# A four-stage layer kernel on one core: local attention with values stationary, Mamba's states by channel halves, a new plan

## Chip, cores, metric

One core of one Trainium2 chip. The metric is the device time of the whole program in microseconds, the median of the runs; lower is better. All times below are microseconds unless they say ns.

## What is computed

16 sequences of 256 tokens, width 128. After a layer norm, the first layer adds a Mamba block and a top-1 mixture of 8 experts to x; after a second layer norm, the second layer adds a 16-head attention with an arccos kernel ("g" units) and a two-deep local-attention transformer ("l" units). What the change touches, cut from the reference:

```python
# Mamba, per channel d (256) and state n (16), along the tokens
h = dA * h + dBx                      # dA = exp(dt*A), dBx = dt*B*x
y = jnp.einsum('bdn,bn->bd', h, c)    # sum over the 16 states
# local attention, 8 heads of 64, window 64, keys of the own and the previous window
sim = jnp.where(mask, -jnp.finfo(sim.dtype).max, jnp.einsum('bhwid,bhwjd->bhwij', bq, bk))
attn = jax.nn.softmax(sim, axis=-1)
out = jnp.einsum('bhwij,bhwjd->bhwid', attn, bv)
x = x + out_reshaped @ wo
```

## The kernel before

The sequences go in 8 pairs (index i or n); a pair has T = 512 tokens, TT = 4 tiles of 128. The work is cut into small units, each with a name: m_* is Mamba, e_* the experts, f_* their joining and second norm, g_* the arccos attention, and the names without a prefix (shift, qkv, norm, qn, heads, score, pt, pv, on, oT, wo, ln, up, gelu, hid, down) the local-attention layer, listed in LAYER. One instance of that layer is one sequence b of a pair in one of the two depths: 8 x 2 x 2 = 32 instances.

**The order.** schedule() is a list scheduler that runs at build time. STAGES gives each unit its engine times, all_units() its due time and what it comes after, LATER and STREAM shift the due times by unit name and by stream. The scheduler hands out the 8 PSUM banks (takes_banks, frees_banks), books a table load on ScalarE (ACT) when a unit needs another activation table (NEEDS, SWITCH), and writes a fixed order for each engine: PE, ACT, DVE, POOL and the DMA queue of SyncE (SP). Each engine then runs its list in order and waits on semaphores.

**Local attention** for one instance (L = 256 tokens, two 128-token tiles, 4 pairs k of heads, z the head of the pair):
- score (L1140, L1144, L1147): scores with queries on partitions. Per head one mask matmul with a bf16 identity, two 64x64 products and one 64x128 product. Four units of it. DVE takes the negative row maximum (L1684, nmx).
- pt (L1155, L1159, L1165, L1166): the same scores transposed, keys on partitions, 320 columns a head (SC). Per head one mask matmul, three products, and two matmuls that add the negative maximum: nmx broadcast as stationary operand, the identity as moving one, 128 and 192 columns. Four units. ACT takes the exponential into PT (L1426); there are two PT tiles for both sequences.
- pv (L1179 to L1181): one unit a head, three matmuls with the exponentials as stationary operand and 65 columns of vv moving: 64 values and a column of ones, which gives the row sum. Eight units.
- on (L1694, L1698): DVE takes the reciprocal of the sums and normalises into oo, three heads at a time.
- oT: eight transposes (L815, the transpose helper) and two ACT copies (L1429) into oT. Then wo (L1195).

**Mamba**, per pair 16 steps k: q, c = divmod(k, 2), so the two channel halves c alternate and q is a pair of states. m_ex (ACT, L1312), m_bx, m_scan, m_hc (DVE, L1530, L1536, L1542), m_sum (PE, L1013), which adds the transposed products into one bank for each half; both banks are taken at the first two steps and given back by m_turn at the end. SP fetches B and C rows, broadcast to 128 partitions, once for each q (512 KB each, L1887 and L1893, 8 + 8 for a pair), into two buffers each; a fetch waits until the steps of q - 2 have read the buffer.

Of the kernel before, what the change touches and what calls it, by code (L numbers as in the profile page):

```python
# [6 lines left out]
ALU = mybir.AluOpType  # L7
# [42 lines left out]
OH = 3  # L50
OG = -(-LH // OH)
# [21 lines left out]
    "g_out": [("PE", 0.89), ("DVE", 0.68)], "out": [("DVE", 0.69), ("SP", 0.1)], "zeros": [("DVE", 0.34)],  # L73
    "shift": [("PE", 0.22), ("ACT", 0.97)], "norm": [("DVE", 0.17), ("ACT", 0.5)], "qn": [("DVE", 1.22)], "heads": [("PE", 0.88), ("ACT", 1.03)],
    "score": [("PE", 1.0), ("DVE", 0.61)], "pt": [("PE", 2.32), ("ACT", 0.7)], "pv": [("PE", 0.64)], "on": [("DVE", 0.78)],
    "oT": [("PE", 0.44), ("ACT", 0.6)], "wo": [("PE", 1.83), ("DVE", 0.42)], "ln": [("PE", 0.69), ("DVE", 0.77), ("ACT", 0.54)],
# [12 lines left out]
         "norm": "ln", "pt": "ln", "ln": "ln", "m_in": "silu", "g_tan": "tan", "gelu": "gelu"}  # L89
SWITCH = 127.0  # L90

LATER = {"down": 9, "e_down": 27, "e_lg": -177, "e_ln": 421, "e_load": -1379, "e_place": 30, "e_pre": -533, "e_route": -824,
         "e_scat": 827, "e_store": -1322, "e_tr": 261, "e_up": 40, "e_xn": -205, "e_xt": -160, "f_ln": 337, "f_tr": -1175,
         "f_xn": 125, "f_yg": 758, "g_av": 86, "g_avT": -766, "g_ev": -1332, "g_hd": -30, "g_ln": 728, "g_norm": -329, "g_oT":
         355, "g_out": 176, "g_pow": 587, "g_qkv": 73, "g_score": 51, "g_sq": 85, "g_sub": 1181, "g_tan": 60, "gelu": -398,
         "heads": 45, "hid": -32, "l_weights": 124, "ln": -103, "ln2": 5, "lnT": -6, "m_B": 636, "m_C": -449, "m_bx": 56,
         "m_dt": 27, "m_du": -6, "m_ex": -11, "m_fin": 286, "m_hc": 82, "m_in": -32, "m_load": 285, "m_out": -1531, "m_scan":
         1342, "m_sum": 17, "m_turn": -313, "m_weights": -862, "m_xp": 1631, "norm": -9, "oT": -3, "on": -102, "out": 152,
         "pt": -29, "pv": 73, "qkv": 47, "qn": -92, "score": -1, "shift": -37, "up": -72, "wo": 32, "x_load": 78, "zeros": 451}

STREAM = {("e", 0): 131, ("e", 1): 87, ("e", 2): 61, ("e", 3): 65, ("e", 4): 580, ("e", 5): 193, ("e", 6): 235,
# [18 lines left out]
         "g_score": 2, "g_avT": 1, "g_oT": 1, "g_out": 1, "shift": 1, "qkv": 1, "heads": 2, "score": 2, "pt": 2, "oT": 1, "wo": 1, "ln": 1,  # L120
         "lnT": 1, "up": 1, "down": 1}
LAYER = ("shift qkv0 qkv2 qkv3 qkv5 norm qn0 heads0 qn1 heads1 score0 score1 pt0 pt1 pv0 pv1 pv2 on0 pv3 score2 score3 "
         "pt2 pt3 pv4 pv5 on1 pv6 pv7 on2 oT0 oT1 wo ln ln2 lnT up0 up1 up2 gelu hid0 hid1 hid2 down")
LAYER = [(x.rstrip("0123456789"), int(x[-1])) if x[-1].isdigit() and x != "ln2" else (x, 0) for x in LAYER.split()]


def durations(unit):
    u, n, b, k = unit
    if u == "e_xt" and n >= GJ[1]:
        return [("PE", 0.11), ("DVE", 0.22)]  # L130
    if u == "e_up" and n >= GJ[1]:
# [25 lines left out]
def all_units():  # L157
# [33 lines left out]
    for n in range(NPAIR):  # L191
# [11 lines left out]
        for q in range(NQ):  # L203
            last = CH * (q - 1) - 1
            unit(t0 + 10 + q, ("m_B", n, 0, q), ("m_xp", n), *[("m_bx", n, 0, last) for z in range(1) if q >= 2])
            unit(t0 + 10 + q, ("m_C", n, 0, q), ("m_xp", n), *[("m_hc", n, 0, last) for z in range(1) if q >= 2])
        for k in range(STEPS):
            q, c = divmod(k, CH)
            t2 = t1 + step * k
            unit(t2 - 4, ("m_ex", n, 0, k), ("m_du", n, 0, c), *[("m_scan", n, 0, k - 2) for z in range(1) if k >= 2])  # L210
            unit(t2, ("m_bx", n, 0, k), ("m_du", n, 0, 0), ("m_du", n, 0, 1), ("m_B", n, 0, q), *[("m_sum", n, 0, k - 2) for z in range(1) if k >= 2])
            unit(t2, ("m_scan", n, 0, k), ("m_bx", n, 0, k), ("m_ex", n, 0, k))
            unit(t2, ("m_hc", n, 0, k), ("m_scan", n, 0, k), ("m_C", n, 0, q))
# [3 lines left out]
        for c in range(CH):  # L217
            unit(t3, ("m_turn", n, 0, c), ("m_sum", n, 0, STEPS - 2 + c))
            unit(t3, ("m_fin", n, 0, c), ("m_turn", n, 0, c))
        unit(t3, ("m_out", n), ("m_fin", n, 0, 0), ("m_fin", n, 0, 1), ("x_load", n))  # L220

    for i in range(NPAIR):
# [45 lines left out]
        for b in range(2):  # L268
            for l in range(LAY):
                n = LAY * i + l  # L270
                for j, (u, k) in enumerate(LAYER):
                    t1 = start + PERIOD * (0.25 * b + 0.5 * l + 0.5 * j / len(LAYER))
                    x = [("zeros", 0, b)]
                    if u == "shift":
                        x = [("down", n - 1, b)] if l else [("f_xn", i)] + [("pt", n - 1, b, 3) for z in range(1) if n]
                    elif u == "qkv":
                        x = [("shift", n, b)] + [("down", n - 1, b) for z in range(1) if n] + [("pv", n - 1, b, 7) for z in range(1) if n and k % 3 == 2]
# [9 lines left out]
                    elif u == "pt":  # L287
                        x = [("score", n, b, k)] + [("pt", n, b, k - 1) for z in range(1) if k]
                    elif u == "pv":
                        x = [("pt", n, b, k // 2), ("qkv", n, b, 2), ("qkv", n, b, 5)] + [("pv", n, b, k - 1) for z in range(1) if k]  # L290
                    elif u == "on":
                        x = [("pv", n, b, z) for z in range(OH * k, min(OH * k + OH, LH))] + [("heads", n, b, z) for z in range(2)]
                    elif u == "oT":
                        x = [("on", n, b, z) for z in range(OG)]
                    elif u == "wo":
                        x = [("oT", n, b, 0), ("oT", n, b, 1)] + [("out", i - 1) for z in range(1) if i and l == 0]
# [15 lines left out]
    for b in range(2):  # L312
        unit(EARLY - 1, ("zeros", 0, b), ("f_yg", 0))
# [11 lines left out]
def bank_of(unit):  # L325
# [13 lines left out]
def takes_banks(unit):  # L339
# [8 lines left out]
    if u == "e_pre" or (u == "e_lg" and n in GP) or (u == "m_sum" and k < CH) or (u == "pv" and k % OH == 0):  # L348
        return (0, 1)
# [3 lines left out]
def frees_banks(unit):  # L353
# [10 lines left out]
    if u == "g_ev":  # L364
        return (-1, ("av", n, b, k))
    if u == "on":
        return (-1, ("o", n, b, k))
# [13 lines left out]
def holds(unit):  # L381
# [137 lines left out]
def shared_before(plan):  # L519

    table = {}
    slot, rb = [(0, 0), (0, 0)], (0, 0)
    for unit in order(plan, "ACT"):
        u, n, b, k = unit
        if u == "pt":
            table[unit] = slot[k % 2]
            slot[k % 2] = (b, LH * n + 2 * k + 2)
# [19 lines left out]
def build(nc, d, out):  # L547
    ctx = ExitStack()
    with ctx:
# [60 lines left out]
        ident_q = sb("ident_q", [P, SC - P])  # L610
        mask_b, maskT_b = sb("mask_b", [P, SQ], BF16), sb("maskT_b", [P, SC], BF16)
# [47 lines left out]
        PT = [sb(f"PT{k}", [P, 2, SC + WIN])[:] for k in range(2)]  # L659
        nmx = [sb(f"nmx{b}", [P, SH, 2])[:] for b in range(2)]  # L660
        rs = [sb(f"rs{b}", [P, 2, OH])[:] for b in range(2)]
# [83 lines left out]
        mask, maskT = PT[0][:, 0, 0:SQ], PT[1][:, 0, 0:SC]  # L745
# [127 lines left out]
        def gpsimd_setup():  # L873
# [12 lines left out]
            for k in range(2):  # L886
                g.memset(PT[k][:, :, SC:], 0.0).then_inc(g_set, 1)
# [1116 lines left out]
```

## Time and profile before

| | |
|---|---|
| median of 3 runs | 2231.11 (2227.65 to 2232.37) |
| span of the profiled execution, the time that the profile has for it | 2227.9 |
| PE, DVE, ACT, POOL busy | 1918.6, 1749.3, 1716.7, 606.3 |
| mean granted TensorE clock | 0.892 |
| activation table loads | 147, 188.6 |
| DMA moved | 126.74 MB |

A busy time is the union of the engine's instructions. Matmuls overlap one another, so the pace of PE is read from the starts of consecutive groups, not from the mean duration. A 32-bit product stands in the trace as two records, a transpose or a bf16 product as one.

### The profile page before, as it was taken

To read this page: it belongs to the slowest core of one execution; us is meant where nothing else is said; L and a number is where in the kernel's file an instruction comes from. 1 tells how busy PE (TensorE), PEld (TensorE's weight loads), DVE (VectorE), ACT (ScalarE), POOL (GpSimd) and SP (SyncE) were. 2 spreads that over 40 slices of the span, in tenths; PEclk is the share of its full clock that TensorE was granted. 3 is DMA by queue.
4 is the path that set the end of the run, shared out by engine and by line. 5 is a ranking of instruction groups with operands and counts; after the bars stand their busy time and mean duration, and the time that the engine had idled before them with its cause. 6 is when DMAs were issued, how large, how long until landed. Compare 5 with 4: busy or idle time off the path is not lost.

```text
span 2227.9 us, 37707 instructions
## 1 busy us (share of the span) xinstructions
PE 1918.6 (86%) x13746; PEld 1454.8 (65%) x13746; DVE 1749.3 (79%) x2649; ACT 1716.7 (77%) x2817; POOL 606.3 (27%) x272
## 2 busy tenths in 40 slices
PE   3677988989897889898889987899789989899997
PEld 2564766778575667667666666667666767676776
DVE  4889897675899889869976799779987898856553
ACT  2446787838887478897888989887888787897987
POOL 2351222222231033421242223403233132313221
PEclk9788888999998988999888998999889998898989
DMA  7651112442111111011200121011100111000000
GB/s 238 223 181 54 48 57 72 131 144 69 59 63 48 49 44 57 30 40 48 67 17 4 49 62 53 11 53 39 62 11 11 62 54 48 1 1 6 1 1 6
DMA packets 67687, 126.74 MB, mean 57 GB/s; under 512 B 8852, under 2 KB 40276, under 8 KB 67380
## 3 DMA queue, kind: packets, MB, share of 16 engines
q1 hardware_dynamic: 61808, 113.19, 16.2%
q0 software_dynamic: 2816, 7.21, 0.9%
q10 hardware_dynamic: 2884, 3.93, 0.5%
q8 instruction: 114, 1.87, 0.4%
q14 instruction: 65, 0.53, 0.1%
HBM read 111.46 MB, written 12.85 MB: 56 GB/s over the span
## 4 chain that ended last, share of the span: by engine, by line
PE 39%; DVE 25%; issue 17%; ACT 14%; DMA 2%; SPq 2%; POOL 0%; DVEq 0%; another core or an unknown queue 0%; ACTq 0%; POOLq 0%
PE ps L815 6%; DVE hB L1536 5%; PE ps L1063 4%; PE ps L1123 3%; DVE hB L1530 3%; PE ps L1159 2%; DVE hB L1542 2%; PE ps L1195 2%; ACT L810 2%; PE ps L1013 2%; PE ps L1166 2%; PE ps L1165 2%; DVE lss L1659 2%; DVE rb L1666 2%; ACT arena L1374 2%
## 5 line engine op out<-in xcount | busy, mean ns | idle before, releaser
L1823 POOL TENSOR_TENSOR arena<-arena 128x1024 f32<-128x1024 f32 x128 | 345.8, 2724 | 755.9 <-ACT arena L1353 755.8
L1827 POOL TENSOR_TENSOR arena<-arena,rb 128x1024 f32<-128x1024 f32 x64 | 166.2, 2596 | 672.0 <-DVE rb L1666 672.0
L1536 DVE TENSOR_TENSOR_SCAN hB<-dA,hB 128x1024 f32<-128x1024 f32 x128 | 316.7, 2479 | 0.7 <-ACT dA L1312 0.5
L815 PE MATMUL ps<-w_ident,arena 128*128 128x128 f32 x879 | 158.4, 333 | 104.9 <-DVE arena L1469 30.7
L815 PEld LDWEIGHTS ps<-w_ident,arena 128*128 128x128 f32 x879 | 127.5, 173 | 136.3 <-issue 81.2
L1374 ACT ACTIVATE arena<-arena 128x256 f32<-128x256 f32 x512 | 205.4, 402 | 2.0
L1312 ACT ACTIVATE dA<-mv,w_A_log 128x510 f32<-128x510 f32 x256 | 168.5, 712 | 49.3 <-DVE hB L1536 48.6
L1123 PE MATMUL ps<-w_l_wqkv,arena 128*128 128x512 f32 x384 | 196.3, 640 | 10.5 <-DVE nmx L1684 6.2
L810 ACT ACT_TABLE_LOAD x147 | 188.6, 1283 | 15.3 <-issue 12.7
L1530 DVE TENSOR_TENSOR hB<-BC,mv 128x1024 f32<-128x1024 f32 x128 | 189.3, 1483 | 13.8 <-PE ps L1013 10.8
L1607 DVE TENSOR_SCALAR arena<-ps 128x1024 f32<-128x1024 f32 x128 | 155.2, 1217 | 40.6 <-PE ps L1063 40.5
L1542 DVE TENSOR_TENSOR hB<-hB,BC 128x1024 f32<-128x1024 f32 x128 | 186.5, 1458 | 0.4
L1013 PE MATMUL ps<-w_ident,hB 128*128 128x128 f32 x1024 | 153.2, 298 | 34.5 <-DVE hB L1542 33.2
L1063 PE MATMUL ps<-gqT,gkT 8*128 8x256 f32 x1024 | 160.6, 460 | 21.6 <-issue 4.2
L1351 ACT ACTIVATE arena<-arena,one_b 128x2048 f32<-128x2048 f32 x64 | 127.9, 1999 | 64.3 <-DVE arena L1607 59.8
L1013 PEld LDWEIGHTS ps<-w_ident,hB 128*128 128x128 f32 x1024 | 129.6, 156 | 53.6 <-DVE hB L1542 43.9
L1426 ACT ACTIVATE PT<-ps 128x640 f32<-128x640 f32 x128 | 89.1, 696 | 73.7 <-PE ps L1166 55.8
L1684 DVE TENSOR_REDUCE nmx<-ps 128x4 f32<-128x512 f32 x128 | 87.5, 684 | 69.9 <-PE ps L1147 69.7
L1166 PE MATMUL ps<-ident_q,nmx 128*128 128x192 f32 x512 | 132.3, 341 | 0.0
L1063 PEld LDWEIGHTS ps<-gqT,gkT 8*128 8x128 f32 x1024 | 97.4, 212 | 51.3 <-issue 34.9
L1353 ACT ACTIVATE arena<-arena,one_b 128x2048 f32<-128x2048 f32 x64 | 128.2, 2003 | 2.1
L1369 ACT ACTIVATE arena<-arena,one_b 128x2048 f32<-128x2048 f32 x64 | 127.7, 1995 | 0.1
(222 smaller groups left out, 4554.6 us busy)
## 6 DMA issues: line engine op xcount, KB each, us to landing
BC<-bc_d SPq DMA_DIRECT2D x128, 512.0 KB
BC<-in_experts SPq DMA_DIRECT2D x16, 514.0 KB
arena<-in_experts SPq DMA_DIRECT2D x15, 514.0 KB
mv<-in_experts SPq DMA_DIRECT2D x15, 514.0 KB, 3.6
arena<-in_x SPq DMA_DIRECT2D x8, 256.0 KB, 5.6
xnT_d<-arena SPq DMA_DIRECT2D x8, 256.0 KB, 4.9
hB<-xnT_d SPq DMA_DIRECT2D x8, 256.0 KB
x<-in_x SPq DMA_DIRECT2D x8, 256.0 KB, 4.0
```

The costliest lines, as they stand in the source:

```text
L810: a.preload_act_table_set(names[0])
L815: return t.transpose(out_, in_, ident[0:k, 0:k])
L1013: e = t.matmul(lb()[:, tt * P:(tt + 1) * P], hB[k % 2][:, j, tt * P:(tt + 1) * P], ident, is_transpose=True, start=q == j == tt == 0, stop ...
L1063: e = t.matmul(lb(z)[:, kt * L:(kt + 1) * L], gkT[32 * hi:32 * hi + GD, hb, kt * P:(kt + 1) * P], gqT[32 * hi:32 * hi + GD, hb], start=Tru ...
L1123: e = t.matmul(lb(z), hT1[b][:, tt * P:(tt + 1) * P], w_lqkv[:, l, (w + z) * INNER:(w + z + 1) * INNER], start=True, stop=True)
L1166: e = t.matmul(lb(z)[:, P:SC], top[1], ident_q[:], start=False, stop=True)
L1312: e = a.activation(dA[k % 2][:, j].rearrange("p (s l) -> p s l", s=2)[:, :, 1:], dtv[:, c].rearrange("p (s l) -> p s l", s=2)[:, :, 1:], A ...
L1374: e = a.activation(part, part, ACT.Exp, scale=-3.2, accum_out=vt[m % 2][:, kt, hi, GD + 2:GD + 3])
L1530: v.tensor_tensor(hB[k % 2], Bb[q % 2], bc(du[:, c:c + 1], [P, NG, T]), ALU.mult).then_inc(v_bx, 1)
L1536: v.tensor_tensor_scan(hf, flat2(dA[k % 2]), hf, 0.0, ALU.mult, ALU.add).then_inc(v_scan, 1)
L1542: v.tensor_tensor(hB[k % 2], hB[k % 2], Cb[q % 2], ALU.mult).then_inc(v_hc, 1)
L1823: g.tensor_tensor(la[m % 2][:, half], la[m % 2][:, half], cl[m % 2][:, half], ALU.subtract).then_inc(g_sub, 1)
```

## The change

1. **Scores.** All products of score are 64 x 64, eight in place of four and two; its mask matmul is four 64 x 64 ones in place of two. pt has two products a head (192 and 128 columns) in place of three, the mask is added after them, and the negative maximum comes by two matmuls of 128 columns marked is_transpose and one plain one of 64 columns.
2. **Values stationary.** OH = 4, OG = 2. A pv unit does four heads: 32 value columns are the stationary operand, the exponentials move (192 and 128 columns), four heads side by side in 32-partition groups of the output, 16 matmuls a unit, two units. The result is already transposed. Row sums come from a new unit rsum (two an instance, 8 matmuls each, a stationary block of ones), which fills one bank; ACT turns it into a reciprocal by Ln and Exp. on is one DVE product of 512 columns for each pv. oT's transposes and copies, the reciprocals, ident_q and the ones column of vv are gone. PT has two tiles for each sequence.
3. **Mamba.** From pair 2 on the 16 steps take all states of half 0, then all of half 1; m_turn of half 0 can come in mid-pair. B and C are fetched for each step (16 + 16 for a pair).
4. **Plan.** New STAGES, LATER and STREAM.

```diff
-OH = 3
-OG = -(-LH // OH)
+OH = 4
+OG = LH // OH
...
+BY_HALF = 2
+def step_of(n, k):
+    if n < BY_HALF:
+        return divmod(k, CH)
+    c, q = divmod(k, NQ)
+    return q, c
+def loads_of(n):
+    return NQ if n < BY_HALF else STEPS
...
-        for q in range(NQ):
-            last = CH * (q - 1) - 1
+        for j in range(loads_of(n)):
+            last = steps_free(n, j) - STEPS * n - 1
...
                 elif u == "score":
-                        t.matmul(lb(z)[:, 0:SQ], ident_b[:], mask_b[:], start=True, stop=False)
+                        for y in range(2):
+                            t.matmul(lb(z)[head_rows(y), 0:SQ], ident_b[head_rows(z), head_rows(z)], mask_b[head_rows(z), y],
+                                     start=True, stop=False)
...
-                        e = t.matmul(lb(z)[:, 0:P], qT[head_rows(z), k, b * L:b * L + P], kT[head_rows(z), k, b * L:b * L + P],
+                    for y in range(2):
+                        for z in range(2):
+                            q0 = b * L + y * WIN
+                            e = t.matmul(lb(z)[head_rows(y), 0:P], qT[head_rows(z), k, q0:q0 + WIN], kT[head_rows(z), k, b * L:b * L + P],
...
                 elif u == "pt":
-                        t.matmul(lb(z)[:, 0:P], top[0], ident, start=False, stop=False)
-                        e = t.matmul(lb(z)[:, P:SC], top[1], ident_q[:], start=False, stop=True)
+                        t.matmul(lb(z)[:, 0:P], top[0], ident, is_transpose=True, start=False, stop=False)
+                        t.matmul(lb(z)[:, SC - P:SC], top[1], ident, is_transpose=True, start=False, stop=False)
+                        e = t.matmul(lb(z)[:, P:SC - P], top[1], ident[:, 0:WIN], start=False, stop=True)
...
+                elif u == "rsum":
+                    for kt, cols, q0 in ((0, slice(0, SC - P), 0), (1, slice(SC - P, SC), P)):
+                        for hi in range(OH):
+                            at = k * L + q0
+                            e = t.matmul(lb()[32 * hi:32 * hi + 32, at:at + cols.stop - cols.start], bc(one_b[:, 0:1], [P, 32]),
+                                         PT[b][hi // 2][:, hi % 2, cols], start=k == kt == 0, stop=k == kt == 1, skip_group_check=True)
...
                 elif u == "pv":
-                    t.matmul(o0, pt[:, 0:P], vv[:, 2 * b, k], start=True, stop=True)
-                    t.matmul(o1, pt[:, P:2 * P], vv[:, 2 * b + 1, k], start=True, stop=False)
-                    t.matmul(o1, pt[:, 2 * P:], vv[:, 2 * b, k], start=False, stop=True).then_inc(p_o[b], 1)
+                    for w in range(2):
+                        for kt, cols, q0 in ((0, slice(0, SC - P), 0), (1, slice(SC - P, SC), P)):
+                            for hi in range(OH):
+                                at = w * L + q0
+                                e = t.matmul(lb()[32 * hi:32 * hi + 32, at:at + cols.stop - cols.start],
+                                             vv[:, 2 * b + kt, OH * k + hi, w * HD:(w + 1) * HD], PT[b][hi // 2][:, hi % 2, cols],
+                                             start=w == kt == 0, stop=w == kt == 1, skip_group_check=True)
-                elif u == "oT":
-                    for j in range(4):
-                        e = transpose(lb()[:, j * P:(j + 1) * P], oo[b][:, k, j * P:(j + 1) * P])
...
                 elif u == "pt":
-                    bb, mm = before[unit]
-                    if mm:
-                        a.wait_ge(p_o[bb], mm)
+                    if OG * n + k // 2:
+                        a.wait_ge(p_o[b], OG * n + k // 2)
+                        a.wait_ge(p_rs[b], OG * n + k // 2)
...
-                elif u == "oT":
-                    a.activation(oT[b][:, :, k * P:(k + 1) * P], lb().rearrange("p (a t) -> p a t", a=4), ACT.Copy).then_inc(a_oT[b], 1)
+                elif u == "rsum":
+                    use(LN_EXP)
+                    a.activation(r_, lb().rearrange("p (g t) -> p g t", g=OG), ACT.Ln).then_inc(a_own, na.up())
+                    a.activation(r_, r_, ACT.Exp, scale=-1.0).then_inc(a_rs[b], 1)
...
                 elif u == "on":
-                    v.reciprocal(r_, o_[:, :, :, LD]).then_inc(v_own, nv.up())
-                    v.tensor_tensor(oo[b].rearrange("p t (h e) -> p t h e", e=LD)[:, :, h0:h0 + m], o_[:, :, :, 0:LD],
-                                    bc(r_.unsqueeze(3), [P, 2, m, LD]), ALU.mult).then_inc(v_oo[b], 1)
+                    v.tensor_tensor(o_, bank(("pv", i, b, k)).rearrange("p (w t) -> p w t", w=2), bc(oT[b][:, 2 * k + 1:2 * k + 2], [P, 2, L]), ALU.mult).then_inc(v_oT[b], 1)
```

## Rows read from the trace of the kernel before

**Rows 1.** The page: busy time and share of the span of each engine.

```profile
PE 1918.6 (86%) x13746; PEld 1454.8 (65%) x13746; DVE 1749.3 (79%) x2649; ACT 1716.7 (77%) x2817; POOL 606.3 (27%) x272
```

**Rows 2.** By stretch: PE, PEld, DVE, ACT, POOL busy, clock, DMA share, GB/s.

```profile
0.00:200.00 200.00, 120.47 (x585) 90.92 (x586) 149.04 (x287) 79.73 (x181) 72.35 (x59) 0.83 0.57 183
200.00:560.00 360.00, 322.01 (x2427) 256.40 (x2426) 269.37 (x493) 260.66 (x398) 84.05 (x35) 0.88 0.29 87
560.00:1900.00 1340.00, 1178.25 (x8482) 881.71 (x8480) 1145.63 (x1528) 1098.66 (x1786) 366.18 (x143) 0.90 0.13 43
1900.00:2228.00 328.00, 297.87 (x2256) 225.80 (x2254) 185.22 (x344) 277.68 (x454) 83.75 (x35) 0.90 0.01 3
```

**Rows 3.** The page: the chain that ended last, by engine.

```profile
PE 39%; DVE 25%; issue 17%; ACT 14%; DMA 2%; SPq 2%; POOL 0%; DVEq 0%; another core or an unknown queue 0%; ACTq 0%; POOLq 0%
```

**Rows 4.** Timeline of PE: start, length, line, tiles; idle time before.

```profile
1005.87 0.63 PE L815 MATMUL ps<-w_ident,gpad 128*128 128x128 f32 x4 [1.77 <-DVE gpad L1599]
...
1023.72 0.43 PE L1155 MATMUL ps<-maskT_b,ident_b 128*128 128x320 bf16 x2
1024.08 0.89 PE L1159 MATMUL ps<-arena 64*128 64x128 f32 x12
1024.90 0.49 PE L1165 MATMUL ps<-w_ident,nmx 128*128 128x128 f32 x2
...
1025.55 0.38 PE L1165 MATMUL ps<-w_ident,nmx 128*128 128x128 f32 x2
1025.77 0.49 PE L1166 MATMUL ps<-ident_q,nmx 128*128 128x192 f32 x2
1026.10 0.38 PE L1201 MATMUL ps<-xd,w_ident 128*128 128x128 f32 x2
...
1027.77 0.38 PE L1140 MATMUL ps<-mask_b,ident_b 128*128 128x256 bf16 x2
1028.08 0.45 PE L1144 MATMUL ps<-arena 64*64 64x128 f32 x8
...
1028.88 1.07 PE L1077 MATMUL ps<-arena,vt 128*32 128x256 f32 x16
1029.88 0.48 PE L1063 MATMUL ps<-gqT,gkT 8*128 8x256 f32 x2
```

**Rows 5.** Timeline of PE, 1012.4 to 1015.8: a pv unit and transposes.

```profile
1012.36 0.33 PE L1179 MATMUL ps<-arena,PT 128*128 128x65 f32 x2
1012.98 1.92 PE L815 MATMUL ps<-w_ident,arena 128*128 128x128 f32 x16
1014.73 0.60 PE L815 MATMUL ps<-w_ident,gpad 128*128 128x128 f32 x4
```

**Rows 6.** Busy time by stretch, columns as in rows 2.

```profile
1006.30:1010.40 4.10, 4.10 (x24) 3.48 (x22) 4.00 (x6) 2.71 (x6) 1.67 (x1) 0.58 0.00 0
1010.40:1016.40 6.00, 6.00 (x63) 5.41 (x62) 2.64 (x6) 5.65 (x11) 0.00 (x0) 1.00 0.00 0
```

**Rows 7.** Groups by line and form: busy, mean ns, idle before and releaser.

```profile
L1698 DVE TENSOR_TENSOR arena<-ps,rs 128x384 f32<-128x384 f32 x64 | 35.7, 558 | 2.2
L1698 DVE TENSOR_TENSOR arena<-ps,rs 128x256 f32<-128x256 f32 x32 | 13.6, 425 | 1.1
L1429 ACT ACTIVATE arena<-ps 128x512 f32<-128x512 f32 x64 | 36.4, 592 | 24.6 <-PE ps L815 24.3
L810 ACT ACT_TABLE_LOAD x147 | 188.6, 1283 | 15.3 <-issue 12.7
```

**Rows 8.** The page: the busiest DMA queue: packets, MB, share of 16 engines.

```profile
q1 hardware_dynamic: 61808, 113.19, 16.2%
```

**Rows 9.** SP's waits for C's buffers (total, times, longest); then groups as rows 7.

```profile
SPq L1892 <- DVE hB L1542: 515.7, 44, 26.9
...
L1530 DVE TENSOR_TENSOR hB<-BC,mv 128x1024 f32<-128x1024 f32 x128 | 189.3, 1483 | 13.8 <-PE ps L1013 10.8 <-issue 2.6
L1536 DVE TENSOR_TENSOR_SCAN hB<-dA,hB 128x1024 f32<-128x1024 f32 x128 | 316.7, 2479 | 0.7 <-ACT dA L1312 0.5
```

More of the change, by code:

```diff
@@ L48 @@
 SH = 4
-OH = 3
-OG = -(-LH // OH)
+OH = 4
+OG = LH // OH
+HD = LD // 2
 H2 = LD // 2
@@ L88 @@
 NEEDS = {"e_ln": "ln", "e_route": "ln", "m_weights": "ln", "m_dt": "ln", "m_ex": "ln", "f_ln": "ln", "g_norm": "ln", "g_ln": "ln", "g_pow": "ln",
-         "norm": "ln", "pt": "ln", "ln": "ln", "m_in": "silu", "g_tan": "tan", "gelu": "gelu"}
+         "norm": "ln", "pt": "ln", "rsum": "ln", "ln": "ln", "m_in": "silu", "g_tan": "tan", "gelu": "gelu"}
 SWITCH = 127.0
[L92 to L99, printed above, removed]
@@ L101 @@
-STREAM = {("e", 0): 131, ("e", 1): 87, ("e", 2): 61, ("e", 3): 65, ("e", 4): 580, ("e", 5): 193, ("e", 6): 235,
[13 rows of a table removed]
+LATER = {"down": 24.763, "e_down": 2.854, "e_lg": -527.923, "e_ln": -47.549, "e_load": -1141.58, "e_place": 301.584, "e_pre": -69.939,
+         "e_route": -96.772, "e_scat": 776.234, "e_store": -1086.84, "e_tr": 123.218, "e_up": 51.438, "e_xn": -39.5, "e_xt": -439.919,
+         "f_ln": 728.245, "f_tr": -1344.64, "f_xn": 897.455, "f_yg": -216.18, "g_av": 84.952, "g_avT": -874.806, "g_ev": -592.979,
+         "g_hd": -36.694, "g_ln": 1158.03, "g_norm": -590.431, "g_oT": 540.373, "g_out": 890.253, "g_pow": 855.006, "g_qkv": 75.94,
+         "g_score": 48.714, "g_sq": -53.184, "g_sub": 477.056, "g_tan": 59.954, "gelu": -933.579, "heads": 42.059, "hid": -87.217,
+         "l_weights": -408.804, "ln": -70.709, "ln2": -5.905, "lnT": -21.866, "m_B": 129.039, "m_C": 197.688, "m_bx": 56.31,
+         "m_dt": 28.089, "m_du": 13.295, "m_ex": -6.828, "m_fin": 363.886, "m_hc": 193.362, "m_in": -48.525, "m_load": -990.542,
+         "m_out": -1640.26, "m_scan": 1257.59, "m_sum": 11.711, "m_turn": -1104.4, "m_weights": -151.849, "m_xp": 1620.41,
+         "norm": 13.735, "on": -767.341, "out": -329.652, "pt": -26.666, "pv": 66.852, "qkv": 46.923, "qn": -34.536, "rsum": -45.212,
+         "score": -2.916, "shift": -208.739, "up": -415.053, "wo": 22.046, "x_load": 375.334}
@@ L127, in durations, with loads_in @@
+def loads_in(n, j):
+    return (sum(loads_of(x) for x in range(n)) + j) // 2 + 1
 def durations(unit):
@@ L136, in durations @@
         return [("POOL", 1.5 * TT * (GP[n + 1] - GP[n]))]
+    if u == "rsum" and k:
+        return STAGES[u] + [("ACT", 1.2)]
     if u == "qkv":
@@ L276, in all_units @@
                     elif u == "qkv":
-                        x = [("shift", n, b)] + [("down", n - 1, b) for z in range(1) if n] + [("pv", n - 1, b, 7) for z in range(1) if n and k % 3 == 2]
+                        x = [("shift", n, b)] + [("down", n - 1, b) for z in range(1) if n] + [("pv", n - 1, b, OG - 1) for z in range(1) if n and k % 3 == 2]
                     elif u == "norm":
@@ L288, in all_units @@
                         x = [("score", n, b, k)] + [("pt", n, b, k - 1) for z in range(1) if k]
+                        x += [(w, n, b, k // 2 - 1) for w in ("rsum", "pv") if k >= 2]
+                    elif u == "rsum":
+                        x = [("pt", n, b, 2 * k + z) for z in range(2)] + [("rsum", n, b, k - 1) for z in range(1) if k]
                     elif u == "pv":
-                        x = [("pt", n, b, k // 2), ("qkv", n, b, 2), ("qkv", n, b, 5)] + [("pv", n, b, k - 1) for z in range(1) if k]
+                        x = [("pt", n, b, 2 * k + z) for z in range(2)] + [("qkv", n, b, 2), ("qkv", n, b, 5)]
+                        x += [("pv", n, b, k - 1) for z in range(1) if k]
                     elif u == "on":
-                        x = [("pv", n, b, z) for z in range(OH * k, min(OH * k + OH, LH))] + [("heads", n, b, z) for z in range(2)]
-                    elif u == "oT":
-                        x = [("on", n, b, z) for z in range(OG)]
+                        x = [("pv", n, b, k), ("rsum", n, b, OG - 1)]
                     elif u == "wo":
-                        x = [("oT", n, b, 0), ("oT", n, b, 1)] + [("out", i - 1) for z in range(1) if i and l == 0]
+                        x = [("on", n, b, z) for z in range(OG)] + [("out", i - 1) for z in range(1) if i and l == 0]
                     elif u == "ln":
@@ L347, in takes_banks @@
         return (1, 1)
-    if u == "e_pre" or (u == "e_lg" and n in GP) or (u == "m_sum" and k < CH) or (u == "pv" and k % OH == 0):
+    if u == "e_pre" or (u == "e_lg" and n in GP) or (u == "m_sum" and step_of(n, k)[0] == 0) or u == "pv" or (u == "rsum" and k == 0):
         return (0, 1)
@@ L365, in frees_banks @@
         return (-1, ("av", n, b, k))
+    if u == "rsum" and k:
+        return (1, ("r", n, b))
     if u == "on":
-        return (-1, ("o", n, b, k))
+        return (-1, ("pv", n, b, k))
     if u == "ln2":
@@ L521, in shared_before @@
     table = {}
[L522 to L527, printed above, removed]
+    rb = (0, 0)
     for unit in order(plan, "DVE"):
@@ L658, in build @@
         lss = sb("lss", [P, TT, 2 * LH])[:]
-        PT = [sb(f"PT{k}", [P, 2, SC + WIN])[:] for k in range(2)]
+        PT = [[None, sb(f"PT{b}", [P, 2, SC])[:]] for b in range(2)]
         nmx = [sb(f"nmx{b}", [P, SH, 2])[:] for b in range(2)]
-        rs = [sb(f"rs{b}", [P, 2, OH])[:] for b in range(2)]
         arena = sb("arena", [P, 19168])
@@ L744, in build @@
         zero = a0.get(DM)
-        mask, maskT = PT[0][:, 0, 0:SQ], PT[1][:, 0, 0:SC]
+        mask, maskT = PT[0][1][:, :, 0:SQ], PT[1][1][:, 0]
         qks = a0.get(LAY, 2, 2, LD)
-        first += [(w_before, d["before"]), (gate, d["gateT"]), (rank, d["rank"]), (mask, d["mask"]), (maskT, d["maskT"])]
+        first += [(w_before, d["before"]), (gate, d["gateT"]), (rank, d["rank"]), (mask, d["mask"].rearrange("p (y c) -> p y c", y=2)), (maskT, d["maskT"])]
         later.append((qks, d["qk_scale"]))
@@ L885, in gpsimd_setup @@
                 g.memset(vt[k][:, :, :, GD + 1:GD + 2], 1.0).then_inc(g_set, 1)
-            for k in range(2):
-                g.memset(PT[k][:, :, SC:], 0.0).then_inc(g_set, 1)
-        all_set = 10
+        all_set = 8
         def vector_setup():
```

184 lines of the change are left out of this document (89 added, 95 removed), and 27 rows, old and new, of the table STREAM.

## The prediction

> **What bounds the kernel now.** I read the busy shares first [rows 1]: PE 1918.6 of 2227.9, but DVE and ACT are close behind, so no single engine explains the span. Then the stretches [rows 2]. From 200 to 560 PE leads by 53 over DVE, from 560 to 1900 by only 33 (1178 against 1146), and from 1900 on by 20 over ACT, while DVE is idle there for 143. Before 200 the kernel waits for loads and for the routing of the experts, which the change hardly touches. Then the chain [rows 3]: PE 39%, DVE 25%, ACT 14%, and 17% "issue", time in which the engine on the chain waited for nothing the profile shows. So the core is bound by three engines in turn: work taken from PE shows in full only where PE leads, and a new order decides the rest.
>
> **PE, part by part.** PE is costed by the distance between starts, at the higher clock level (these rows lie in stretches of granted clock 1.00).
>
> *pt.* One unit runs from 1023.72 to 1026.10, 2.38 [rows 4]: masks 0.36, products 0.82, maxima 1.20. The products keep their 320 columns a head but are four matmuls, not six. Lower bound 0.55 (a 128-column step takes 0.22 and a 192-column one 0.33, and the two heads overlap), upper bound 0.82 as now; I take 0.65. Of the maxima, a head has two transposing steps and one of 64 columns. 16 transposes take 1.75 [rows 5], 0.11 each. The 64-column step lies between 0.11 and the 0.21 that each of the three 65-column steps of pv takes (0.62 for the three [rows 5]); I take 0.21, the nearest row. Two heads: 2 x (0.11 + 0.11 + 0.21) = 0.86. The unit comes to 0.36 + 0.65 + 0.86 = 1.87, a gain of 0.5 (0.3 to 0.8). Four an instance: 2.0 (1.2 to 3.2).
>
> *score.* 1027.77 to 1028.88, 1.11 [rows 4]: masks 0.31, the two groups of products 0.80. The second group takes the form of the first and should cost no more than its half, 0.40 or a little less. The masks are quarter blocks: if the four overlap as the 64x64 products do, 0.15; if not, 0.31 or a little more. I take 0.15, with 0.78 for the products, and so a gain of 0.2 (-0.1 to 0.5), 0.8 an instance (-0.4 to 2.0).
>
> *pv and oT.* Eight heads at 0.62 is 5.0, eight transposes at 0.11 is 0.9 [rows 5]: 5.9 goes. The new pv has the shape of L1077 (128 rows, 32 columns): there 8 matmuls of 256 columns take 1.00 [rows 4], so four column groups do overlap. pv moves 2560 columns, L1077 2048: 1.25 a unit; rsum moves 1280: 0.63. Two of each: 3.8. The gain is 2.1 (1.7 to 2.5). The Trainium skill, TensorEngine Tiling, Key Properties, says that a change of tiling mode drains the engine, which speaks against many small pv and rsum units among full-width work. By that rule each unit would pay again on entry; the starts around L1077, with both of its neighbours in another mode, already hold it, so the sum would be the same unless rsum, the shorter unit, pays the whole drain a second time.
>
> Together 4.9 an instance (2.5 to 7.7), times 32 is 157 (80 to 246) at the full clock. The mean granted clock is 0.892: 157 / 0.892 = 176 of PE's busy time (90 to 276). PE would come to about 1743.
>
> **DVE.** on loses 64 products of 384 columns and 32 of 256 (35.7 + 13.6) [rows 7], 49 in all, and 96 small reciprocals that I leave out. It gains 64 products of 512 columns. From 425 at 256 and 558 ns at 384 columns, 133 ns for 128 columns, one is 0.69: 44. DVE comes to 1744, 5 less, and lower by the reciprocals. **ACT.** 64 copies of 592 ns go, 36.4 [rows 7]; 32 Ln of the same 512 columns from PSUM and 32 Exp of the same size come, at the same 0.59 each, 38. ACT stays at 1718. But the copies ran under any table and the new pair needs Ln and Exp: from none to two loads of 1.283 each time [rows 7], 0 to 82. pt's exponential stands directly before in the instance and needs the same table, so I take 0. Should other work come between, this cover is gone.
>
> **The hand-offs.** The end of an instance was reciprocal, product, eight transposes, two copies, wo; it is now two products of 0.69 and wo, with Ln and Exp beside the second pv. Against this, the third pt exponential now waits for rsum and pv of the first four heads together (1.9 of PE behind the second exponential), where before it waited for two heads. Two instances run side by side and PE has other work; I cost both at nothing. If cover is missing, the wait costs 1.9 an instance, 61 in all.
>
> **Mamba.** The operations are the same. Freed: one of eight PSUM banks for most of six pairs. Its worth shows in no row, since a wait for a bank is charged to the bank's reader; it lies between 0 and the 162 for which PE idles in the middle stretch [rows 2], nearer to 0, since most waits there are for data. I count it as part of the new plan. Added: 6 x 16 = 96 fetches of 512 KB. Queue q1 moved 113.19 MB in 16.2% of the span, 361 [rows 8], 1.67 a fetch, 161 in total spread over some 1500 in which the DMA engines stand at 13% [rows 2]: hidden. On SP each is queued behind a wait for its buffer. SP waits 516 for C's buffers [rows 9], so fetches start as soon as a buffer falls free; m_bx idled 10.8 for PE and for no DMA. Two buffers now cover two steps, not four: a fetch has one whole step of DVE to land at the tightest, 2.48 + 1.48 and as much again for m_hc, 5.4 [rows 9], and on average (1900 - 60) / 128 = 14. I cost it at nothing; m_bx and the scan, and all that DVE has behind them, wait if it fails.
>
> **The sum.** With nothing reordered, each stretch gains at most PE's lead plus what DVE loses [rows 2]: 200 to 560 takes 176 x 360/2028 = 31, under its lead of 53; 560 to 1900 its lead of 33 and 3 of DVE's; after 1900 its lead of 20. That is 87. By the chain, PE and its issue time are 56% of 2228 [rows 3], and 176/1919 of that is 114. At the far end a plan that rebalances everything gives the whole 176. As the plan is made anew and the leads of the long middle stretch are small and local, I take the middle of 114 and 176 less a little: 125. Span 2228 - 125 = 2103; the median of the runs stands 3 above this span, so 2106.
>
> **Rivals.**
> - *Half the gain is eaten by the clock and by unmoved bounds.* From 1006.3 to 1010.4 PE was granted 0.58 of its clock, mostly the lower level of 1.2 GHz, after it had idled 1.8 [rows 4], and the pt unit that fills this stretch took 4.1 [rows 6] where the other took 2.38. A PE with more gaps has more such stretches. If the mean falls from 0.892 to 0.85, PE's work of (1919 x 0.892 - 157)/0.85 is 1829, a cut of 90, and the time falls by 60 to 2170. Chance 0.22.
> - *No change: pt's transposes lower the clock.* pt now holds 512 of them. If they let the clock fall to 0.58 during each pt, a unit takes 1.87 / 0.58 = 3.2, 1.4 more, 173 in all, and the gain is gone: about 2230. Against it: 20 transposes in a row [rows 5] lie in a stretch at 1.00 [rows 6]. Chance 0.03. The Trainium skill, TensorE: Matmul & The Clock Gate, part 4, says that transposes do not count as busy for the gate; by that rule this rival would be the likely one, and the row just named speaks against it.
> - *The plan gets all of it*, pairs overlap more tightly and the freed bank pays: 176 and 15 more, 2040. For: DVE idles 143 in the last stretch [rows 2]. Against: three engines at 1720 to 1745 each are hard to fill. Chance 0.13.
> - *Slower: B and C land late.* Place: DVE's in-order list at m_bx and m_hc in pairs 2 to 7. The 96 added fetches each cost the time by which they miss; at 125 / 96 = 1.3 each the gain is gone, and at 1.8 the time is 2106 + 173, about 2279. SP has to reach each fetch in time, and its list also holds waits for the output. Against: no row shows DVE waiting for a fetch. Chance 0.05.
> - *The column groups of pv do not overlap* as L1077's do, since their weights come from one tile: then the 48 matmuls of pv and rsum at 0.22 to 0.33, 13 an instance in place of 3.8, put PE 330 higher than forecast, at 2073, and at its share of before, 86%, the time is 2400. Chance 0.03.
> - My forecast, 2106, with own range 2060 to 2155: 0.54.
>
> **The numbers.** A measurement of this kernel can tell about 0.2%, 4.5, from no change. Faster: 0.54 + 0.22 + 0.13 = 0.89; same 0.03; slower 0.05 + 0.03 = 0.08. The range goes from 2035, the full cut, to 2185, the clock rival at a third of the gain; it leaves out the late fetches and what little lies below.
>
> **What would show it.** PE's busy time at 1720 to 1790, pt at 1.8 to 2.0 from start to start, pv at 1.2 to 1.3, rsum near 0.63, DVE about 1730 to 1745, ACT about 1718 with 140 to 155 table loads, and a mean granted clock of 0.87 to 0.90. DVE idle before m_bx for BC <- bc_d would show the late fetches; a clock under 0.86 the first rival; PE's busy share still at 86% of the shorter span the full cut. I am wrong in kind if PE falls as computed and the span does not follow by at least 60.

## The result: slower, with the profile after

The changed kernel takes 2286.76 (2282.23 to 2294.02, 4 runs), the kernel before beside it 2231.68: ratio 1.0245, 95% interval 1.0213 to 1.0278. It is 55 slower, where 2106 was forecast. The busy times and the chain in the page of the changed kernel, against [rows 1, 3]:

```profile
span 2284.4 us, 40458 instructions
...
PE 1785.2 (78%) x15282; PEld 1287.8 (56%) x15282; DVE 1760.1 (77%) x2517; ACT 1728.0 (76%) x2822; POOL 609.4 (27%) x270
...
PE 35%; DVE 24%; ACT 21%; issue 15%; DMA 3%; SPq 2%; POOL 0%; DVEq 0%; ACTq 0%; POOLq 0%
```

PE lost 133 of busy time, at a mean granted clock of 0.856 in place of 0.892. Busy time times clock gives an estimate of the work at the full clock: 1785 x 0.856 = 1528 against 1919 x 0.892 = 1711, a cut of 183. So PE has less to do, as intended, and yet the span grew by 57. No engine is above 78%. On the chain ScalarE went from 14% to 21%.

The timeline of PE in the changed kernel shows the new units one after the other (start, length, line, tiles), in place of [rows 4, 5]:

```profile
566.64 0.82 PE L1190 MATMUL ps<-arena 64*128 64x192 f32 x8
567.39 0.45 PE L1193 MATMUL ps<-maskT_b,ident_b 128*128 128x320 bf16 x2
567.67 0.27 PE L1198 MATMUL ps<-w_ident,nmx 128*128 128x128 f32 x1
567.78 0.27 PE L1199 MATMUL ps<-w_ident,nmx 128*128 128x128 f32 x1
567.89 0.33 PE L1200 MATMUL ps<-w_ident,nmx 128*128 128x64 f32 x2
...
568.45 1.11 PE L1008 MATMUL ps<-mv,hB 128*128 128x128 f32 x8
```

```profile
570.39 0.30 PE L1169 MATMUL ps<-mask_b,ident_b 64*64 64x256 bf16 x4
570.52 0.39 PE L1174 MATMUL ps<-arena 64*64 64x128 f32 x8
570.74 0.39 PE L1179 MATMUL ps<-arena 64*64 64x128 f32 x8
571.06 1.13 PE L1091 MATMUL ps<-gqT,gkT 8*128 8x256 f32 x8
572.12 0.36 PE L1211 MATMUL ps<-arena,one_b 128*32 128x192 f32 x2
...
572.80 0.30 PE L1169 MATMUL ps<-mask_b,ident_b 64*64 64x256 bf16 x4
...
573.47 0.36 PE L1223 MATMUL ps<-arena 128*32 128x192 f32 x2
...
574.69 1.16 PE L1130 MATMUL ps<-w_g_outT,avS 128*128 128x128 f32 x8
```

A pt unit takes 568.45 - 566.64 = 1.81 (before 2.38), a score unit 571.06 - 570.39 = 0.67 (before 1.11), rsum 0.68, pv 1.22.

**Where the time is lost.** Mamba's pairs follow one another, so the start of each pair's first scan is a milestone. From the starts of the scan in both traces:

```
pair             0     1     2     3     4     5     6     7   last end
before          65   216   604   786  1021  1260  1502  1754   2228
changed         65   226   670   822  1078  1322  1529  1815   2284
```

Pair 2 starts 66 late, and from there to the end the changed kernel needs 1614 against 1624. The second expert phase lies before pair 2; its last tile is done at 570 against 548, so 22 are lost by then, and where they go was not traced. Then 100 pass to the scan, where the kernel before needs 56: the other 44. The timelines of the changed kernel, PE first and then ACT and DVE, show what the 100 are spent on:

```profile
597.79 1.96 PE L1026 MATMUL ps<-mv,w_x_projT 128*96 128x512 f32 x4
```

```profile
598.52 1.91 ACT L1400 ACTIVATE arena<-arena 128x2048 f32<-128x2048 f32 x1
600.34 1.89 ACT L1397 ACTIVATE arena<-arena 128x2048 f32<-128x2048 f32 x1
602.26 1.91 ACT L1400 ACTIVATE arena<-arena 128x2048 f32<-128x2048 f32 x1
604.19 1.28 ACT L842 ACT_TABLE_LOAD   x1
605.49 1.19 ACT L1483 ACTIVATE arena<-ps,w_l_b 128x256 f32<-128x256 f32 x3
606.70 1.28 ACT L842 ACT_TABLE_LOAD   x1
...
631.90 2.00 ACT L1389 ACTIVATE arena<-arena,one_b 128x2048 f32<-128x2048 f32 x1
633.93 2.00 ACT L1391 ACTIVATE arena<-arena,one_b 128x2048 f32<-128x2048 f32 x1
...
640.01 0.58 ACT L1325 ACTIVATE hB<-ps 96x512 f32<-96x512 f32 x1
...
670.50 2.28 DVE L1578 TENSOR_TENSOR_SCAN hB<-dA,hB 128x1024 f32<-128x1024 f32 x1
```

PE has the product of m_xp ready at 599.8; the 0.58 copy that Mamba waits for (L1325) comes at 640.0, behind 40 of arccos attention, feed-forward work and table loads in ACT's list. In the kernel before the same copy follows its product by 2, at 582:

```profile
578.29 1.96 PE L998 MATMUL ps<-mv,w_x_projT 128*96 128x512 f32 x4
```

```profile
582.17 0.57 ACT L1287 ACTIVATE hB<-ps 96x512 f32<-96x512 f32 x1
```

The shift of m_xp itself is nearly the same in both kernels (1631 and 1620); what the other shifts put before it is not. Busy time by stretch of the changed kernel, columns as in [rows 2]:

```profile
560.00:600.00 40.00, 39.55 (x407) 29.91 (x406) 27.84 (x75) 34.67 (x59) 16.54 (x12) 1.00 0.12 33
600.00:640.00 40.00, 31.03 (x121) 18.21 (x119) 19.60 (x33) 38.81 (x70) 11.78 (x6) 0.79 0.01 3
640.00:671.00 31.00, 19.83 (x186) 13.57 (x187) 20.90 (x20) 25.99 (x38) 8.29 (x4) 0.67 0.35 110
```

From 600 to 640 ACT is full, DVE half idle, and PE drops to 31 at a clock of 0.79: PE idles from 603.4 for 3.2, and the lower clock level sets in at 605.4. The activations shown take what they took before (2.00 for L1389, as L1351 then); the copy stands too late in the list.

### The profile page after: what moved, and what is told of

Its sections match the earlier page's. It is cut to its first block, busy times and chain, and to the rows that moved or that the text cites. A ratio compares the mean times of both kernels' runs of the same rounds, so it can differ in the third digit from the quotient of the medians.

```text
span 2284.4 us, 40458 instructions
## 1 busy us (share of the span) xinstructions
PE 1785.2 (78%) x15282; PEld 1287.8 (56%) x15282; DVE 1760.1 (77%) x2517; ACT 1728.0 (76%) x2822; POOL 609.4 (27%) x270
## 4 chain that ended last, share of the span: by engine, by line
PE 35%; DVE 24%; ACT 21%; issue 15%; DMA 3%; SPq 2%; POOL 0%; DVEq 0%; ACTq 0%; POOLq 0%
PE ps L847 4%; DVE hB L1578 4%; ACT arena L1412 4%; PE ps L1091 4%; PE ps L1151 3%; ACT L842 3%; PE ps L1041 3%; DVE hB L1572 2%; ACT arena L1407 2%; PE ps L1190 2%; DVE hB L1584 2%; DVE arena L1718 2%; DVE lss L1701 2%; ACT arena L1397 2%; DVE rb L1708 2%
## 5 line engine op out<-in xcount | busy, mean ns | idle before, releaser
L847 PE MATMUL ps<-w_ident,arena 128*128 128x128 f32 x623 | 118.3, 340 | 131.0 <-DVE arena L1511 30.0
L1151 PE MATMUL ps<-w_l_wqkv,arena 128*128 128x512 f32 x384 | 206.5, 670 | 15.9 <-DVE rb L1708 8.3
L1572 DVE TENSOR_TENSOR hB<-BC,mv 128x1024 f32<-128x1024 f32 x128 | 180.7, 1414 | 29.7 <-PE ps L1041 29.3
L1041 PE MATMUL ps<-w_ident,hB 128*128 128x128 f32 x1024 | 160.0, 308 | 47.6 <-DVE hB L1584 47.3
L847 PEld LDWEIGHTS ps<-w_ident,arena 128*128 128x128 f32 x623 | 90.3, 175 | 162.2 <-issue 103.3
L1584 DVE TENSOR_TENSOR hB<-hB,BC 128x1024 f32<-128x1024 f32 x128 | 178.5, 1399 | 0.3
L1389 ACT ACTIVATE arena<-arena,one_b 128x2048 f32<-128x2048 f32 x64 | 127.9, 1998 | 35.3 <-DVE arena L1649 20.6
L1190 PE MATMUL ps<-arena 64*128 64x192 f32 (+1 forms) x1024 | 113.8, 344 | 29.1 <-DVE nmx L1726 12.0
L1151 PEld LDWEIGHTS ps<-w_l_wqkv,arena 128*128 128x128 f32 x384 | 75.3, 214 | 97.3 <-issue 89.6
```

The costliest lines, as they stand in the source:

```text
L847: return t.transpose(out_, in_, ident[0:k, 0:k])
L1041: e = t.matmul(lb()[:, tt * P:(tt + 1) * P], hB[k % 2][:, j, tt * P:(tt + 1) * P], ident, is_transpose=True, start=q == j == tt == 0, stop ...
L1151: e = t.matmul(lb(z), hT1[b][:, tt * P:(tt + 1) * P], w_lqkv[:, l, (w + z) * INNER:(w + z + 1) * INNER], start=True, stop=True)
L1572: v.tensor_tensor(hB[k % 2], Bb[j % 2], bc(du[:, c:c + 1], [P, NG, T]), ALU.mult).then_inc(v_bx, 1)
L1584: v.tensor_tensor(hB[k % 2], hB[k % 2], Cb[j % 2], ALU.mult).then_inc(v_hc, 1)
```

## Experiments

Two theories. **Order**: the units gain, but the shifts LATER and STREAM make a poor order of them. **Units**: the new attention or the Mamba halves cost more than they save. Ratios are to the kernel before, timed beside each run; to compare with the changed kernel, divide by its 1.0245. The medians of the kernel before lie between 2231 and 2244 from session to session, so times of different sessions are compared by their ratios. Each kernel keeps its own STAGES, the costs that the scheduler reckons with; what they are worth was not tried.

**The shifts exchanged.** First the changed units with the old shifts:

```diff
-LATER = {"down": 24.763, "e_down": 2.854, "e_lg": -527.923, ...
+LATER = {"down": 9, "e_down": 27, "e_lg": -177, ... "rsum": 0}
```

> The changed units, with the due-time shifts (LATER, STREAM) of the kernel before; rsum gets a shift of 0. Theory 'order': the changed kernel is slow because its new shifts make a poor order of the work, not because of its units. Then shifts that were never fitted to these units do no worse than the new ones: 2230 to 2275. Theory 'units': the new local attention, or the Mamba halves with a fetch for each step, costs more than it saves, whatever the order. Then shifts fitted to other units come on top: 2300 or more.

Measured: ratio 1.0093 (1.0062 to 1.0125), 2263. Shifts that were never fitted to these units beat the ones made for them by 1.5%. Then the old units with the new shifts:

```diff
-LATER = {"down": 9, "e_down": 27, "e_lg": -177, ...
+LATER = {"down": 24.763, "e_down": 2.854, "e_lg": -527.923, ... "oT": -45.212, "zeros": 0}
```

> The units of the kernel before, unchanged, with the due-time shifts of the changed kernel (oT takes the shift of rsum). Theory 'order': the new shifts are a poor order for any units, so over 2290. Theory 'units': the shifts as such are sound and only the units are slow, so within 20 of 2231.

Measured: 1.0359 (1.0286 to 1.0433), 2322. Both as the theory "order" had it. An exchange also mismatches shifts and units, so the next runs take the shifts away.

**No shifts, part by part.** In these four LATER and STREAM are empty; e5 has BY_HALF = 8, so that Mamba runs as before; e6 is the kernel before with the Mamba part put in.

```diff
-LATER = {"down": 9, ...
-STREAM = {("e", 0): 131, ...
+LATER = {}
+STREAM = {}
```

> The kernel before with all shifts zero: the scheduler goes by the plain due times. This is the neutral order for the units of before; alone it only shows what the shifts are worth. Both theories expect a kernel much slower than 2231, 2400 to 2550.

> The changed kernel with all shifts zero, against e3_before_no_shifts: the units compared with no fitted order on either side. Theory 'order': the new units are faster by 70 to 180 than those of before. Theory 'units': they are not faster, the difference is under 20 or of the other sign.

> The changed local attention alone: Mamba's steps alternate the halves again in all pairs, with 8 + 8 fetches each (BY_HALF = 8), all shifts zero. e3_before_no_shifts gave 2456 for the units of before, e4_after_no_shifts 2333 for both changes. Theory 'attention': the local attention carries the gain between them, so this is at 2310 to 2360. Rival 'Mamba': the freed bank carries a good part of it, so 2380 or more; third case, the per-step fetches cost and eat a part, so under 2310.

> Mamba's halves and the fetch for each step alone, on the local attention of before, all shifts zero. Theory 'attention': within 30 of the 2456 of e3_before_no_shifts. Rival 'Mamba': 2420 or less. If the late fetches of the prediction are real, 2500 or more, with DVE waiting at m_bx for BC <- bc_d.

| no shifts | ratio (95%) | PE busy | clock |
|---|---|---|---|
| e3, units of before | 1.0946 (1.0901 to 1.0992) | 1988 | 0.852 |
| e6, Mamba part alone | 1.0929 (1.0892 to 1.0967) | 1958 | 0.859 |
| e5, attention alone | 1.0603 (1.0560 to 1.0646) | 1815 | 0.843 |
| e4, both | 1.0397 (1.0357 to 1.0437) | 1783 | 0.851 |

With no fitted order on either side the changed units are faster by 1.0946 - 1.0397 = 5.5%, 123 (2456 to 2333), at the same clock. The attention gives 3.4% alone. Mamba's halves alone give 0.2%, which their intervals of 0.4% do not tell from nothing, and 2.1% on top of the attention. e5, at 2370, is 10 above the range for "attention carries all". The theory "units" is out. And the shifts are worth 9.5% to the kernel before, 212 (2456 against the 2244 beside it), and 1.5% (1.0397 to 1.0245), 34, to the changed one.

**What a microsecond is worth.** 256 extra mask matmuls in each kernel's own order, then 64 Arctans left out (the arccos attention has wrong values):

```diff
+                        t.matmul(lb(z)[:, 0:SC], ident_b[:], maskT_b[:], start=True, stop=True)
...
-                    a.activation(at, at, ACT.Arctan).then_inc(a_own, na.up())
```

> The kernel before with each of pt's 256 mask matmuls issued twice (the first is overwritten), in the unchanged order: 128 x 0.33 = 42 us of PE at the full clock, some 47 at the granted one. It asks what a microsecond of PE is worth on the old order. If PE is on the path for more than half of the time: +25 to +45 over the kernel before.

> The same 256 extra matmuls in the changed kernel, in its own order. Theory 'order' says that PE is no longer what this order waits for, so they cost clearly less than in e9_before_extra_mask: 0 to +20 over the changed kernel's 2287. Rival 'PE still binds': as much as in e9_before_extra_mask.

> The kernel before with the Arctan of g_tan left out (64 activations of 1.995, 128 us of ScalarE; the arccos attention then has wrong values), in the unchanged order. What ScalarE is worth on the old order: 14% of the chain, so 30 to 60 less.

> The same in the changed kernel: the Arctan of g_tan left out, 128 us of ScalarE less in its own order. Theory 'order', as the chain has it (21% ScalarE in place of 14%): the new order waits for ScalarE, so this gains clearly more than e11_before_no_atan does, 60 to 110. Rival: no more than there.

Measured: e9 1.0147 (1.0114 to 1.0179), so the extra work, estimated at 42 and seen in PE's busy time as 33 (1951.9), cost 33. e10 1.0249 (1.0227 to 1.0272) against the 1.0245 of the changed kernel: 1, with some 9 of uncertainty, for 27 more of PE's busy time (1811.7). e11 1.0045 (1.0029 to 1.0061): 116 less of ACT bought nothing in the old order (30 to 60 was expected, a miss; it is even slightly slower). e12 1.0076 (1.0051 to 1.0100), 1.7% or 38 under the changed kernel, less than the 60 to 110 expected. The page of e12, busy times and chain:

```profile
PE 1780.7 (79%) x15282; PEld 1284.8 (57%) x15282; DVE 1757.0 (78%) x2517; ACT 1610.9 (72%) x2758; POOL 611.7 (27%) x270
...
PE 36%; DVE 25%; ACT 18%; issue 15%; DMA 3%; SPq 2%; POOL 0%; DVEq 0%; ACTq 0%; POOLq 0%
```

Added PE work lengthens the old order and not the new one; ACT work taken out shortens the new order and not the old one. So in the new order PE's saved time shows as idle time. That PE work taken out of the old order would pay as much as added work costs was not tried.

**One place mended.**

```diff
         want[what] = time + LATER.get(what[0], 0.0) + STREAM.get(stream(what), 0.0)
+        if what[0] == "m_xp" and what[1] == 2:
+            want[what] -= 1600
```

> The changed kernel with one due time moved: the unit m_xp of pair 2 is due 1600 earlier; the rest of the order is what the scheduler then makes of it. In the changed kernel m_xp's copy out of PSUM starts 47 us after its Silu inputs are done, and Mamba's pair 2 starts 66 us later than in the kernel before. Theory 'one place': pair 2 starts at 600 to 630 in place of 670 and the whole time falls by 30 to 66, to 2220 to 2257. Rival 'everywhere': pair 2 starts earlier but the time is lost again behind it, less than 20 gained, over 2267.

Measured: 1.0083 (1.0057 to 1.0110), 1.6% or 36 under the changed kernel. Its timeline of DVE has pair 2's first scan at 621, not 670:

```profile
613.85 2.36 DVE L1574 TENSOR_TENSOR hB<-BC,mv 128x1024 f32<-128x1024 f32 x2
621.15 4.33 DVE L1580 TENSOR_TENSOR_SCAN hB<-dA,hB 128x1024 f32<-128x1024 f32 x1
```

The scheduler makes the rest of the order anew behind the moved unit, so the 49 won there do not simply carry through: by the starts of the scans in both traces the lead over the changed kernel is 49, 20, 56, 36, -34 and 14 at pairs 2 to 7. At the end it is 36, with some 9 of uncertainty. So one due time, with what the scheduler then makes of the rest, gives back about two thirds of the 55.

**The shifts fitted anew**, by many small random steps in LATER and STREAM that were kept when the scheduler's plan got shorter. The searches start from different shifts: e7 and e8 from those of the changed kernel, e14 and e16 from those of the kernel before. Nothing else is changed (e8 and e15 have BY_HALF = 8).

```diff
-LATER = {"down": 24.763, "e_down": 2.854, "e_lg": -527.923, ...
+LATER = {"down": 19.544, "e_down": -43.655, "e_lg": -293.473, ...
```

> The changed kernel, its units untouched, with LATER and STREAM found anew by some thousands of small random steps from the ones it has, kept when the scheduler's own plan gets shorter. Theory 'order': the shifts it came with were simply poor, so this is faster than both kernels: 2170 to 2222. Rival 'cannot be used': with PE, DVE and ACT at nearly equal work no order helps, or the scheduler's costs miss what the chip does with the new units; then over 2230.

> The changed local attention with Mamba's steps as before (BY_HALF = 8), shifts found anew in the same way from those of the changed kernel. If the attention alone carries the gain: 2190 to 2235. If it needs the freed bank as well: 2240 or more.

> The changed kernel with shifts from a second, longer search, begun from those of the kernel before. If e7_after_refit's 2213 was an early stop and a good order carries the unit gain of the unfitted kernels (123 us) in full, 2110 to 2180. If the order is near its end, as three engines of about the same work leave little to gain: 2195 to 2220.

> The changed local attention, Mamba's steps as before (BY_HALF = 8), shifts from an equally long search. If Mamba's halves are worth something in a fitted order: 15 or more above e14_after_refit2. If not: within 15 of it.

> The kernel before with shifts from an equally long search from its own. If its order was fitted to the end: within 10 of 2231. If any order could be bettered so: 2215 or less, and the gain of e7_after_refit would say nothing of the units.

| fitted shifts | ratio (95%) | median |
|---|---|---|
| e16, units of before, again | 1.0012 (0.9980 to 1.0044) | 2241 |
| e8, attention alone, short search | 1.0049 (1.0024 to 1.0074) | 2247 |
| e14, both, longer search | 0.9923 (0.9888 to 0.9957) | 2225 |
| e7, both, short search | 0.9893 (0.9860 to 0.9925) | 2213 |
| e15, attention alone, longer search | 0.9862 (0.9838 to 0.9886) | 2207 |

The search found nothing for the old units. It made the changed kernel faster than both kernels: e7, with other shifts alone, is 1.1% under the kernel before, and e15, the new attention without the Mamba part, 1.4%. Both gains are clear of the noise and under 2%. e14 came out no better than e7: 2225 lies 5 above the 2195 to 2220 of "near its end", far from the 2110 to 2180 of the full gain, and its runs spread from 2203 to 2240. e8 alone would have said that the attention needs the freed bank; e15, the same units after a longer search, says that it does not. It came out 18 below e14, where "within 15" was expected. e8 and e15 differ by 1.9% with the same units, more than e15 and e14 do, so no value of the Mamba part in a fitted order is shown. Page of e15, busy times and chain:

```profile
PE 1752.1 (79%) x15282; PEld 1263.7 (57%) x15282; DVE 1747.8 (79%) x2517; ACT 1713.4 (78%) x2812; POOL 622.6 (28%) x270
...
PE 32%; DVE 27%; ACT 19%; issue 17%; DMA 3%; SPq 2%; POOL 0%; DVEq 0%; ACTq 0%; POOLq 0%
```

Three engines stand at 78 to 79% of the span, where PE alone stood at 86% [rows 1].

## Why the prediction was wrong

*The units were right, and a little better than costed.* pt 1.81 (1.87 forecast), score 0.67 (0.93 forecast; the quarter masks overlap, 0.13 for the four, and so do the products of the two groups, 0.54 for both), pv 1.22 (1.25), rsum 0.68 (0.63). PE's cut is 183 at the full clock where 157 was forecast. The column groups overlap: pv's 2560 columns in 1.22. So the rival without overlap is out.

*DVE.* The new product of on takes 682 ns, as forecast, and with the reciprocals gone the units cost DVE less (42 against 49 and 18 for the reciprocals), but its total rose by 11:

```profile
L1732 DVE TENSOR_TENSOR arena<-ps,arena 128x512 f32<-128x512 f32 x64 | 42.3, 682 | 24.5 <-ACT arena L1471 20.4 <-PE ps L1223 3.8
...
L1718 DVE TENSOR_TENSOR arena<-arena,lss 128x1024 f32<-128x1024 f32 x64 | 115.5, 1833 | 8.0 <-ACT lss L1449 7.6
```

L1718, the product of qn, which the change does not touch, takes 1833 ns where it took 1249, 38 in all. The traces show where: of its 64 instances 39 lie beside no addition of POOL and take at most 1.23 each, and 25 overlap one and take 2.80 on average, up to 3.40. In the kernel before only 2 of 64 overlap one. Such a pair in the changed kernel, with the next instance alone behind it, DVE first and then POOL:

```profile
803.11 3.40 DVE L1718 TENSOR_TENSOR arena<-arena,lss 128x1024 f32<-128x1024 f32 x1
806.43 0.28 DVE L1641 TENSOR_TENSOR gpad<-gqk,gpad 128x128 f32<-128x128 f32 x1
806.63 1.21 DVE L1718 TENSOR_TENSOR arena<-arena,lss 128x1024 f32<-128x1024 f32 x1
```

```profile
803.07 2.35 POOL L1856 TENSOR_TENSOR arena<-arena,rb 128x1024 f32<-128x1024 f32 x1 [5.34 <-DVE rb L1708]
```

No run moved POOL's work, and what the 38 are worth to the span was not measured. Table loads went from 147 to 152, within the forecast; the five more cost 6, not 82.

*The hand-offs*, costed at nothing, show no added waiting: DVE idles 24.5 before on, most of it for ACT's reciprocal (the line above), where it idled 27.7 before the reciprocals and products of the old on. pt's exponentials idle 64 in all, where they idled 74.

*Late fetches, the slower rival.* Its price, 2279, lies near the measured time by luck, since its mechanism is absent: m_bx idled for PE and not for a fetch, and e6, the fetches and halves alone, is not slower than e3.

```profile
L1572 DVE TENSOR_TENSOR hB<-BC,mv 128x1024 f32<-128x1024 f32 x128 | 180.7, 1414 | 29.7 <-PE ps L1041 29.3
```

*The clock, the first rival.* It fell to 0.856, as that rival said. It does not explain the loss: e3 and e4 stand at 0.852 and 0.851 and still differ by 123, and in the stretch 600 to 640 PE idles first. What the lower clock adds to the time is not shown. *Transposes and the clock:* the pt unit above, with its four transposes 0.11 apart, lies in the stretch 560 to 600 at 1.00, so they did not lower the clock. The Trainium skill, TensorE: Matmul & The Clock Gate, part 4, says that full speed does not engage for transposes, which do not count as busy in the same way. That is not seen here, where other matmuls stand around them; no run has transposes alone.

*The step that failed* is in the sum: "As the plan is made anew and the leads of the long middle stretch are small and local, I take the middle of 114 and 176 less a little: 125." It took for granted that the new order fits the new units at least as well as the old order fitted the old ones. The change brings some 160 new shifts, and no row of before tells what they are worth; I priced them at a gain and gave no rival in which the order itself makes the kernel slower.

The runs showed in its place that this term outweighs any unit: the shifts take 212 off the units of before (e3) and only 34 off the changed ones (e4), 178 less, and that turns the 123 of the units into a loss of 55. The step also has a slip of its own: the middle of 114 and 176 is 145, so 125 is 20 less, with no row for it. With no shifts on either side the units gave 123; that this is near 125 is luck, since 125 was worked out from a fitted order.

Even in a good order 125 would have been wrong: e7 gave 24 and e15, without the Mamba part, 31. e16's search found no room in the old order, and e9 shows that added PE work cost it nearly in full. Why so little of the 123 is left in a fitted order stays open; that PE, DVE and ACT, level at 1713 to 1752 in e15, each wait for the others is argued and not shown. The first estimate, each stretch's lead of PE alone, 87, was nearer, and still about three times too high.

## What to carry to other kernels

Where a hand-tuned or searched order is part of a change, price it as a part of its own, in both directions: here the order was worth 212 to the units of before and 34 to the changed ones, the units 123. Compare units with no fitted order on either side, and fit both before judging; a saving on an engine shows only if the order waits for that engine, and a few extra instructions (e9, e10) give a sign of that in one run. In the trace, look for a short instruction at the head of a long chain that stands in an engine's list long after its input is ready: here it was a 0.58 copy, 40 late, and moving its due time forward gave back about two thirds of the loss.

## What the runs showed that I had not expected

Four bf16 mask matmuls of 64 x 64 and 256 columns take 0.13 between starts of the groups, where two full ones took 0.31 [rows 4]. Taking 116 of ScalarE work out of the kernel before made it 0.45% slower (e11); that work which ends earlier meets other work at a worse moment is a guess, which no trace was read for. A product of DVE that takes 1.22 alone takes up to 3.40 beside an addition of POOL. And the same kernel can spread: e14's 12 runs range over 37, e15's 5 over 10.
